# Causal attention of many small heads: every product of the groups in four column tiles, masks included

## The chip, the cores and the metric

One core of one Trainium2 chip runs the whole program. The metric is the device time in microseconds; the kernel before was timed in three runs.

## The reference

`x` is (2, 2048, 256) in f32, and the attention has 16 heads of 16 columns. Cut to what matters:

```python
Q, K, V = (proj(Wq), proj(Wk), proj(Wv))          # x @ W.T, split into 16 heads of 16
scores = scale * einsum('bhtd,bhsd->bhts', Q, kb)  # causal: -inf where s > t
m_new = maximum(m, max(scores)); p = exp(scores - m_new)
acc = corr * acc + einsum('bhts,bhsd->bhtd', p, vb)
x = layernorm(x + O @ Wo.T)
x = layernorm(x + int8_product(x, rhs))            # rows of x and columns of rhs quantised to 127
```

## The kernel before

**Groups.** The 32 heads (2 batches of 16) are worked through in 8 groups of 4 heads. The queries of a group lie in 4 chunks of 512 columns, the keys in 16 blocks of 128. Q and K are split into three bf16 parts and stacked, so that one bf16 product over 96 rows gives a score in f32 quality. Three more rows carry the negative maximum of each query, so that the product of scores (99 rows) already has it subtracted.

**Two kinds of product.** The *maxima* are made first: an item `(i, b, w, h)` of `ITEMS` is the product of the 128 queries of tile `i` with `w` keys of block `b`, for two heads (`PAIR`). It fills one of two slots (`MAX_SLOTS`) of two PSUM banks; VectorE reduces it to block maxima (L975). An item on the diagonal (`diag`, `b == i // TPC`) is 128, 256, 384 or 512 wide and gets a second matmul behind its product (L705), which adds -1e30 above the diagonal of its last 128 columns: `ident_b` times `mask_q`. A group has 80 items, 32 of them on the diagonal. The *scores* are made later, in 40 steps `(c, kb)` of `STEPS`, each for four heads: keys of one block in the rows, up to 512 queries in the columns (384, 256 and 128 in the last three steps of a chunk). They go through three PSUM banks; ScalarE takes the exponential into `PR` (L927). GpSimd cuts the diagonal (L1197).

**Values.** Two steps later (`LAG`) the four heads' values are multiplied in f32: four matmuls side by side in the four column tiles of the array, 32 columns of weights each, into one bank (L728). The trace shows an f32 matmul as two.

**Forms.** A matmul with 128 columns of weights uses the whole array. `product` can cut it into four matmuls with 32 columns of weights each (`QUADS`, `QW`), one beside the other in the four column tiles. Before, `in_quads` says which: 384 columns and wider, and never an item on the diagonal. So non-diagonal items (all 512 wide) and scores of 512 and 384 columns go in quarters (L688); diagonal items, their masks and scores of 256 and 128 columns go whole (L686, L705).

**Order.** TensorE's order is written out ahead by `quota`. It runs over the steps with a clock counted in columns, gives each product at least `LOAD` = 256 columns and each change of form `FORM` = 288, and places the next item behind a score when the item's slot is free. The stream of a *steady* group (the first six) is the items from 46 (`AHEAD`) on of its own, and the items before 46 of the next; the seventh (*full*) makes all 80 of the last group too, 114 in all; the last one makes none and has the end of the layer (projection, norms, integer product) beside it. In a steady group the planner finds a place for each item with the slot free when TensorE comes to it; in the seventh it has to let TensorE come up to 1024 columns earlier. When a chunk's items are done, TensorE turns the maxima (L713, whole), ScalarE negates them, GpSimd splits them into three parts and SP loads them into the stack (`TURNS`).

**Front.** Before the groups the weights and `x` are turned and projected; the first 46 items of group 0 lie in between (`FRONT_QUOTA`).

Of the kernel before, what the change touches and what calls it, by code (L numbers as in the profile page):

```python
# [26 lines left out]
P = 128  # L27
# [8 lines left out]
CH = 512  # L36
TPC = CH // P
# [4 lines left out]
MAX_SLOTS = 2  # L42
PAIR = 2
# [25 lines left out]
def build(nc, x, wq, wk, wv, wo, ffn, out):  # L69
# [8 lines left out]
    STACK = len(Q_TERMS) * DH  # L78
    KROWS = STACK + PARTS
# [8 lines left out]
    ITEMS = [(i, b, min(CH, P * (i + 1) - CH * b), h)  # L88
             for i in range(TILES) for b in range(i // TPC + 1) for h in range(HG // PAIR)]
    NI = len(ITEMS)  # L90
    ITEM_COLS = [PAIR * w for _, _, w, _ in ITEMS]
# [3 lines left out]
    skip = lambda c, kb: P * max(0, kb - TPC * c)  # L95
# [10 lines left out]
        full=[(0, n) for n in range(AHEAD, NI)] + [(1, n) for n in range(NI)],  # L106
        last=[])

    QUADS, WIDE = 4, 384
    QW = P // QUADS  # L110
    in_quads = lambda w, diag=False: w >= WIDE and not diag

    LAG, BATCH = 2, 1
    FORM, LOAD, READ, READ_FROM = 288, 256, 2.5, 340

    def quota(stream):

        made = lambda m: PAIR * (max(ITEM_COLS[m] // PAIR, LOAD) + (P if ITEMS[m][1] == ITEMS[m][0] // TPC else 0))  # L120
        read = lambda m: READ_FROM + READ * ITEM_COLS[m]

        def place(pace, early):
            at, done, free, seen, n, out, quads = 0, 0, [0] * MAX_SLOTS, 0, 0, [], True
            for k, (c, kb) in enumerate(STEPS):
                out.append([])
                for j in range(HG):
                    at += max(CH - skip(c, kb), LOAD) + FORM * (quads != in_quads(CH - skip(c, kb)))
                    quads = in_quads(CH - skip(c, kb))
                    if n < len(stream) and free[n % MAX_SLOTS] <= at + early and seen * pace <= at:  # L130
                        i, b, w, _ = ITEMS[stream[n][1]]
                        at = max(at, free[n % MAX_SLOTS]) + made(stream[n][1]) + FORM * (quads != in_quads(w, b == i // TPC))
                        quads = in_quads(w, b == i // TPC)
                        done = max(done, at) + read(stream[n][1])
                        free[n % MAX_SLOTS] = done
                        seen += read(stream[n][1])
                        n += 1
                    out[k].append(n)
                if k % BATCH == BATCH - 1:
                    at += FORM * (not quads)  # L140
                    quads = True
                    at += sum(HG * (CH - skip(*STEPS[k - back])) for back in range(LAG, LAG + BATCH))
            return out if n == len(stream) else None

        return next(out for early in range(0, 16 * CH, CH // 2) for pace in range(160, -1, -2)
                    for out in [place(pace / 100, early)] if out) if stream else [[0] * HG for _ in STEPS]
# [17 lines left out]
    FRONT_QUOTA, n, seen = [], 0, 0  # L164
# [77 lines left out]
    with ExitStack() as ctx:  # L242
# [9 lines left out]
        ident_b = sb("ident_b", [P, P], BF16)  # L252
        ones = sb("ones", [P, P], F32)
        mask_q = sb("mask_q", [P, P], BF16)
# [10 lines left out]
        QS = QS_words[:, :].bitcast(BF16).rearrange("p (s c j n) -> p s c j n", s=2, c=CHUNKS, j=HG)  # L265
        KS = sb("KS", [KROWS, 2, CHUNKS, HG, CH], BF16)
# [143 lines left out]
        with nc.Block() as block:  # L410
# [172 lines left out]
            def _(pe):  # L583
# [69 lines left out]
                def front():  # L653
                    pe.wait_ge(ready, 1)
                    turn_weights(0)
                    turn_x(0, 0)
                    turn_weights(1)
                    turn_x(0, 1)
                    turn_weights(2)
                    done = 0  # L660
                    for n in range(XCHUNKS):
                        for u in range(UNITS_X):
                            if n == 0 and u in (0, 2, 4):
                                pe.wait_ge(w_copied, u // 2 + 1)
                            unit(n, u)
                            if n == 0 and u == 3:
                                turn_weights(3)
                                turn_weights(4)
                            if n == 1 and u == 2:
                                ffn_weights()  # L670
                            if u in (1, 3) and n + 1 < XCHUNKS:
                                turn_x(n + 1, u // 2)
                            for m in range(done, FRONT_QUOTA[n][u]):
                                if m == 0:
                                    pe.wait_ge(ready, 2)
                                    pe.wait_ge(f_copied, 2)
                                item(0, 0, m)
                            done = FRONT_QUOTA[n][u]
                        if n == FRONT_TURN:
                            turn_first_maxima()  # L680

                def product(bank, w, stack, moving, quads, stop=True):


                    if not quads:
                        return pe.matmul(bank[:, 0:w], stack, moving, start=True, stop=stop)  # L686
                    for t in range(QUADS):
                        m = pe.matmul(bank[t * QW:t * QW + QW, 0:w], stack[:, t * QW:t * QW + QW], moving,  # L688
                                      start=True, stop=stop)
                    return m  # L690

                def item(q, p, n):

                    i, b, w, h = ITEMS[n]
                    if n in FIRST_ITEM:
                        pe.wait_ge(s_qs[p][i // TPC], SL * (q + 1))
                        pe.wait_ge(s_ks[p][i // TPC], SL * (q + 1))
                    at_least(pe, s_reduced, item_use(2 * q + p, n) - MAX_SLOTS + 1)
                    diag = b == i // TPC
                    for t in range(PAIR):  # L700
                        bank, j = ps_max[:, n % MAX_SLOTS * PAIR + t, :], h * PAIR + t
                        m = product(bank, w, QS[0:STACK, p, i // TPC, j, i % TPC * P:i % TPC * P + P],
                                    KS[0:STACK, p, b, j, 0:w], in_quads(w, diag), stop=not diag)
                        if diag:
                            m = pe.matmul(bank[:, w - P:w], ident_b[:, :], mask_q[:, :], start=False, stop=True)  # L705
                    m.then_inc(s_piece, 1)

# [24 lines left out]
                def group(q, p):  # L732
                    g, kind = 2 * q + p, KIND(2 * q + p)
                    first = isinstance(g, int) and g == 0
                    groups = [(q, p), (q, 1) if p == 0 else (q + 1, 0)]
                    n = 0
                    for k, (c, kb) in enumerate(STEPS):
                        s = skip(c, kb)
                        if kb == 0:
                            pe.wait_ge(s_qs[p][c], SL * (q + 1))  # L740
                            pe.wait_ge(s_ks[p][c], SL * (q + 1))
                            pe.wait_ge(s_mrow[c], 16 * PARTS * (g + 1))
                        for j in range(HG):
                            pos = unit_pos(kind, k, j)
                            at_least(pe, s_exp, score_base(g) + pos - behind(pos) + 1)
                            bank = ps_score[:, score_slot(pos), :]
                            product(bank, CH - s, KS[:, p, kb // TPC, j, kb % TPC * P:kb % TPC * P + P],
                                    QS[0:KROWS, p, c, j, s:CH], in_quads(CH - s)).then_inc(s_st, 1)
                            while n < QUOTA[kind][k][j]:
                                on, m = STREAM[kind][n]  # L750
                                item(*groups[on], m)
                                n += 1
                            if kind == "last" and j % 2:
                                project(k, j // 2)
                        if kind == "last":
                            end_parts(k)
                        if k >= LAG:
                            values(g, k - LAG, kind)
                        elif not first:
                            values(g - 1, NS + k - LAG, KIND(g - 1))  # L760
                        for at, on, tc in TURNS[kind]:
                            if at == k:
                                pos = turn_pos(kind, on, tc)
                                turn_maxima(g + on, tc, score_base(g) + pos, pos)
# [546 lines left out]
```

## Time and profile before

| | |
|---|---|
| median of three runs | 1074.32 us (1074.15 to 1074.58) |
| profiled execution | 1081.22 us |
| its span | 1079.5 us |
| TensorE, matmuls | 1014.5 us, 94% |
| VectorE | 826.0 us, 77% |
| ScalarE | 716.4 us, 66% |
| mean granted clock of TensorE | 0.978 |

The span is the stretch from the first to the last instruction of the profiled execution. A matmul's length in the timeline includes its way through the array, so lengths overlap; how fast matmuls follow each other is read from their starts. "PEld" is the loading of weights, "96*32" the rows and columns of the weights, "96x512" the rows and columns that stream past them. A line "x8" merges eight instructions: its length is from the first start to the last end.

### The profile page before, as it was taken

Reading aid. Unit: us, or ns where it says so; the run is one execution under the profiler, and the core shown is the slowest. Engines: PE = TensorE matmul, PEld = TensorE weight load, DVE = VectorE, ACT = ScalarE, POOL = GpSimd, SP = SyncE. Lnnn points to the kernel's source line nnn. Section 1 sums busy time; section 2 is a strip of 40 time slices with the busy share of each in tenths; the row PEclk is TensorE's granted clock in tenths of the full one; section 3 lists DMA queues with packets and bytes.
Section 4 is the critical chain, followed back from the end, with each engine's and each line's share of the span. In section 5 each row is a group of like instructions: output and inputs, shape, how many; then the busy total and the mean of one; then the engine's idle time right before and its main releaser. Section 6 shows DMA issues by size and latency. Waiting matters only on the chain.

```text
span 1079.5 us, 27959 instructions
## 1 busy us (share of the span) xinstructions
PE 1014.5 (94%) x11656; PEld 416.3 (39%) x11656; DVE 826.0 (77%) x1083; ACT 716.4 (66%) x1471; POOL 264.0 (24%) x435
## 2 busy tenths in 40 slices
PE   8999999999999999999999999999999899999872
PEld 5554433333333333333333333334333333434331
DVE  4566667877787778777877778777788898499697
ACT  3444477677767787777777777777766466677640
POOL 3534520112011201120112011101211101565644
PEclk9999989999999999999999999999999999999995
DMA  5656510003010301030103011201120410315501
GB/s 165 189 165 214 160 26 7 8 2 86 21 37 9 85 16 38 10 87 12 38 18 84 7 37 29 74 7 42 33 70 8 118 41 2 97 53 151 154 30 49
DMA packets 71810, 66.88 MB, mean 62 GB/s; under 512 B 15112, under 2 KB 65608, under 8 KB 71684
## 3 DMA queue, kind: packets, MB, share of 16 engines
q1 hardware_dynamic: 71684, 65.10, 21.5%
q8 instruction: 92, 1.51, 0.6%
q14 instruction: 34, 0.28, 0.1%
HBM read 43.25 MB, written 21.35 MB: 60 GB/s over the span
## 4 chain that ended last, share of the span: by engine, by line
PE 81%; DVE 10%; ACT 4%; DMA 2%; issue 1%; SPq 1%; POOL 1%; POOLq 0%; DVEq 0%; ACTq 0%
PE ps_acc L728 21%; PE ps_score L688 18%; PE ps_max L688 15%; PE ps_max L686 8%; DVE block_max L975 6%; PE ps_score L611 5%; ACT PR L927 3%; PE ps_score L686 3%; PE ps_max L705 3%; PE ps_score L618 3%; PE ps_max L802 2%; DMA end_slots<-heads_out 1%; PE ps_acc L592 1%; DVE stats L1089 1%; DMA row_sums<-accS 1%
## 5 line engine op out<-in xcount | busy, mean ns | idle before, releaser
L975 DVE TENSOR_REDUCE block_max<-ps_max 128x2 f32<-128x1024 f32 (+3 forms) x640 | 658.5, 1062 | 196.8 <-PE ps_max L688 108.4
L927 ACT ACTIVATE PR<-ps_score 128x512 f32<-128x512 f32 (+3 forms) x1280 | 628.1, 537 | 229.0 <-PE ps_score L688 142.4
L688 PE MATMUL ps_score<-QS,KS 99*32 99x512 bf16 (+1 forms) x4096 | 347.4, 377 | 12.8 <-ACT PR L927 10.6
L728 PE MATMUL ps_acc<-PR,VG 128*32 128x512 f32 (+3 forms) x2560 | 295.4, 536 | 0.0
L688 PE MATMUL ps_max<-KS,QS 96*32 96x512 bf16 x3072 | 236.1, 383 | 10.9 <-DVE block_max L975 8.5
L1197 POOL TENSOR_SCALAR_AFFINE_SELECT PR<-PR 128x512 f32<-128x512 f32 x128 | 81.6, 638 | 456.3 <-ACT PR L927 456.3
L688 PEld LDWEIGHTS ps_score<-QS,KS 99*32 99x32 bf16 x4096 | 104.7, 95 | 202.4 <-ACT PR L927 94.4
L686 PE MATMUL ps_max<-KS,QS 96*128 96x384 bf16 (+3 forms) x512 | 128.8, 305 | 3.5 <-DVE block_max L975 2.8
L688 PEld LDWEIGHTS ps_max<-KS,QS 96*32 96x32 bf16 x3072 | 68.8, 96 | 109.2 <-DVE block_max L975 51.8
L705 PE MATMUL ps_max<-mask_q,ident_b 128*128 128x128 bf16 x512 | 102.8, 221 | 0.0
L728 PEld LDWEIGHTS ps_acc<-PR,VG 128*32 128x32 f32 x2560 | 68.0, 109 | 49.2 <-issue 10.6
L686 PEld LDWEIGHTS ps_max<-KS,QS 96*128 96x128 bf16 x512 | 48.9, 98 | 97.0 <-issue 45.2
L611 PE MATMUL ps_score<-PR,wT 128*128 128x512 f32 x128 | 62.3, 613 | 0.7 <-ACT neg_max L889 0.7
L686 PE MATMUL ps_score<-QS,KS 99*128 99x256 bf16 (+1 forms) x256 | 54.7, 257 | 3.3 <-ACT PR L927 1.7
L1184 POOL TENSOR_TENSOR end_slots<-PR,end_slots 128x512 bf16<-128x512 f32 x32 | 37.0, 1157 | 70.0 <-ACT end_slots L876 70.0
L686 PEld LDWEIGHTS ps_score<-QS,KS 99*128 99x128 bf16 x256 | 21.2, 98 | 84.0 <-ACT PR L927 70.6
L871 ACT CAST end_slots<-ps_score 128x512 bf16<-128x512 f32 x32 | 18.8, 586 | 49.4 <-PE ps_score L611 49.4
L705 PEld LDWEIGHTS ps_max<-mask_q,ident_b 128*128 128x128 bf16 x512 | 50.4, 99 | 2.8 <-issue 2.3
L1205 POOL CAST max_parts<-neg_max 16x128 bf16<-16x128 f32 (+1 forms) x31 | 8.8, 285 | 127.4 <-ACT neg_max L910 125.8
L1189 POOL COPY VG<-V 128x256 f32<-128x256 f32 x32 | 12.7, 396 | 87.3 <-PE ps_acc L728 87.0
L611 PEld LDWEIGHTS ps_score<-PR,wT 128*128 128x128 f32 x128 | 22.4, 192 | 24.8 <-issue 24.0
L618 PE MATMUL ps_score<-wT,PR 128*128 128x256 f32 x128 | 31.0, 387 | 0.0
(126 smaller groups left out, 550.1 us busy)
## 6 DMA issues: line engine op xcount, KB each, us to landing
QS<-qparts SPq DMA_DIRECT2D x192, 64.0 KB, 2.4
KS<-kparts SPq DMA_DIRECT2D x192, 64.0 KB, 2.4
qparts<-end_slots SPq DMA_DIRECT2D x16, 384.0 KB, 5.0
kparts<-end_slots SPq DMA_DIRECT2D x16, 384.0 KB, 4.6
PR<-in_L_attn_x SPq DMA_DIRECT2D x8, 512.0 KB, 4.6
heads_out<-accS SPq DMA_DIRECT2D x124, 32.0 KB
end_slots<-in_L_attn_x SPq DMA_DIRECT2D x4, 512.0 KB, 9.5
out_y<-end_slots SPq DMA_DIRECT2D x8, 256.0 KB, 2.1
```

The lines of the kernel that those rows point to most:

```text
L611: m = pe.matmul(bank, wT[:, w, mh, nh * P:nh * P + P], xT[:, n % 2, mh, :], start=mh == 0, stop=mh == HALVES - 1)
L618: m = pe.matmul(bank[:, t * D:t * D + D], xT[:, n % 2, mh, tile * P:tile * P + P], wT[:, 2, mh, :], start=mh == 0, stop=mh == HALVES - 1)
L686: return pe.matmul(bank[:, 0:w], stack, moving, start=True, stop=stop)
L688: m = pe.matmul(bank[t * QW:t * QW + QW, 0:w], stack[:, t * QW:t * QW + QW], moving, start=True, stop=stop)
L705: m = pe.matmul(bank[:, w - P:w], ident_b[:, :], mask_q[:, :], start=False, stop=True)
L728: m = pe.matmul(ps_acc[EYE * j:EYE * j + EYE, s:CH], VG[:, kb, j, :], PR[:, k % 4, j, 0:CH - s], start=kb == 0, stop=k == LAST[c])
L802: y = pe.matmul(ps_max[:, s, t * D:t * D + D], o_in(m)[:, h, at:at + P], wT[:, 3, h, :], start=h == 0, stop=h == HALVES - 1)
L871: act.copy(parts[:, n % 2, u, 0, :], ps_score[:, u % 3, :]).then_inc(part1, 1)
L927: act.activation(PR[:, k % 4, j, 0:w], ps_score[:, score_slot(pos), 0:w], ACT.Exp, scale=SCALE).then_inc(s_exp, 1)
L975: dve.tensor_reduce(block_max[:, h * PAIR:h * PAIR + PAIR, i, b], ps_max[:, slot_at:slot_at + PAIR, 0:w], AX.X, ALU.max).then_inc(s_reduce ...
L1184: pool.tensor_tensor(parts[:, n % 2, u, 2, :], rest[:, q % RESTS, :], parts[:, n % 2, u, 1, :], ALU.subtract).then_inc(part3, 1)
L1197: pool.affine_select(out=block, in_=block, compare_op=ALU.is_ge, fill=0.0, base=0, pattern=[[0, HG], [1, P]], channel_multiplier=-1).then_ ...
```

## The change

All products of the groups go in quarters, whatever their width, and the mask of a diagonal item goes in quarters too. Quarter `r` of the mask covers the rows from `r` and the columns from its own diagonal on, so the four are 128, 96, 64 and 32 columns wide. The items in the front stay whole (`quads=False`). The planner loses the price of a change of form and counts a mask as `LOAD` = 256 columns instead of 128; with this its order shifts by an item here and there, and two turns of maxima of a steady group come one step later (22 to 23, 29 to 30).

```diff
--- before.py
+++ after.py
@@ -106,39 +106,33 @@
         full=[(0, n) for n in range(AHEAD, NI)] + [(1, n) for n in range(NI)],
         last=[])
 
-    QUADS, WIDE = 4, 384
+    QUADS = 4
     QW = P // QUADS
-    in_quads = lambda w, diag=False: w >= WIDE and not diag
 
     LAG, BATCH = 2, 1
-    FORM, LOAD, READ, READ_FROM = 288, 256, 2.5, 340
+    LOAD, READ, READ_FROM = 256, 2.5, 340
 
     def quota(stream):
 
 
 
-        made = lambda m: PAIR * (max(ITEM_COLS[m] // PAIR, LOAD) + (P if ITEMS[m][1] == ITEMS[m][0] // TPC else 0))
+        made = lambda m: PAIR * (max(ITEM_COLS[m] // PAIR, LOAD) + (LOAD if ITEMS[m][1] == ITEMS[m][0] // TPC else 0))
         read = lambda m: READ_FROM + READ * ITEM_COLS[m]
 
         def place(pace, early):
-            at, done, free, seen, n, out, quads = 0, 0, [0] * MAX_SLOTS, 0, 0, [], True
+            at, done, free, seen, n, out = 0, 0, [0] * MAX_SLOTS, 0, 0, []
             for k, (c, kb) in enumerate(STEPS):
                 out.append([])
                 for j in range(HG):
-                    at += max(CH - skip(c, kb), LOAD) + FORM * (quads != in_quads(CH - skip(c, kb)))
-                    quads = in_quads(CH - skip(c, kb))
+                    at += max(CH - skip(c, kb), LOAD)
                     if n < len(stream) and free[n % MAX_SLOTS] <= at + early and seen * pace <= at:
-                        i, b, w, _ = ITEMS[stream[n][1]]
-                        at = max(at, free[n % MAX_SLOTS]) + made(stream[n][1]) + FORM * (quads != in_quads(w, b == i // TPC))
-                        quads = in_quads(w, b == i // TPC)
+                        at = max(at, free[n % MAX_SLOTS]) + made(stream[n][1])
                         done = max(done, at) + read(stream[n][1])
                         free[n % MAX_SLOTS] = done
                         seen += read(stream[n][1])
                         n += 1
                     out[k].append(n)
                 if k % BATCH == BATCH - 1:
-                    at += FORM * (not quads)
-                    quads = True
                     at += sum(HG * (CH - skip(*STEPS[k - back])) for back in range(LAG, LAG + BATCH))
             return out if n == len(stream) else None
 
@@ -674,12 +668,12 @@
                                 if m == 0:
                                     pe.wait_ge(ready, 2)
                                     pe.wait_ge(f_copied, 2)
-                                item(0, 0, m)
+                                item(0, 0, m, quads=False)
                             done = FRONT_QUOTA[n][u]
                         if n == FRONT_TURN:
                             turn_first_maxima()
 
-                def product(bank, w, stack, moving, quads, stop=True):
+                def product(bank, w, stack, moving, quads=True, stop=True):
 
 
                     if not quads:
@@ -689,7 +683,7 @@
                                       start=True, stop=stop)
                     return m
 
-                def item(q, p, n):
+                def item(q, p, n, quads=True):
 
                     i, b, w, h = ITEMS[n]
                     if n in FIRST_ITEM:
@@ -700,8 +694,12 @@
                     for t in range(PAIR):
                         bank, j = ps_max[:, n % MAX_SLOTS * PAIR + t, :], h * PAIR + t
                         m = product(bank, w, QS[0:STACK, p, i // TPC, j, i % TPC * P:i % TPC * P + P],
-                                    KS[0:STACK, p, b, j, 0:w], in_quads(w, diag), stop=not diag)
-                        if diag:
+                                    KS[0:STACK, p, b, j, 0:w], quads, stop=not diag)
+                        if diag and quads:
+                            for r in range(0, P, QW):
+                                m = pe.matmul(bank[r:r + QW, w - P + r:w], ident_b[:, r:r + QW], mask_q[:, r:P],
+                                              start=False, stop=True)
+                        elif diag:
                             m = pe.matmul(bank[:, w - P:w], ident_b[:, :], mask_q[:, :], start=False, stop=True)
                     m.then_inc(s_piece, 1)
 
@@ -745,7 +743,7 @@
                             at_least(pe, s_exp, score_base(g) + pos - behind(pos) + 1)
                             bank = ps_score[:, score_slot(pos), :]
                             product(bank, CH - s, KS[:, p, kb // TPC, j, kb % TPC * P:kb % TPC * P + P],
-                                    QS[0:KROWS, p, c, j, s:CH], in_quads(CH - s)).then_inc(s_st, 1)
+                                    QS[0:KROWS, p, c, j, s:CH]).then_inc(s_st, 1)
                             while n < QUOTA[kind][k][j]:
                                 on, m = STREAM[kind][n]
                                 item(*groups[on], m)
```

## Rows read from the trace of the kernel before

**Rows 1.** Busy time of each engine over the span, from the page.

```profile
PE 1014.5 (94%) x11656; PEld 416.3 (39%) x11656; DVE 826.0 (77%) x1083; ACT 716.4 (66%) x1471; POOL 264.0 (24%) x435
```

**Rows 2.** The chain that ended last, by engine and by line.

```profile
PE 81%; DVE 10%; ACT 4%; DMA 2%; issue 1%; SPq 1%; POOL 1%; POOLq 0%; DVEq 0%; ACTq 0%
PE ps_acc L728 21%; PE ps_score L688 18%; PE ps_max L688 15%; PE ps_max L686 8%; DVE block_max L975 6%; PE ps_score L611 5%; ACT PR L927 3%; PE ps_score L686 3%; PE ps_max L705 3%; PE ps_score L618 3%; PE ps_max L802 2%; DMA end_slots<-heads_out 1%; PE ps_acc L592 1%; DVE stats L1089 1%; DMA row_sums<-accS 1%
```

**Rows 3.** A steady group, the seventh and the eighth: length, busy us (instructions), clock, DMA share, GB/s.

```profile
core 0: us, PE busy (x) PEld busy (x) DVE busy (x) ACT busy (x) POOL busy (x), PEclk, DMA share, GB/s
459.90:566.40 106.50, 105.36 (x1381) 40.63 (x1381) 83.29 (x85) 80.95 (x169) 17.12 (x36) 1.00 0.14 37
779.70:917.50 137.80, 125.54 (x1589) 46.64 (x1588) 116.92 (x125) 83.49 (x169) 17.54 (x37) 0.99 0.19 49
917.50:1045.40 127.90, 116.34 (x1062) 51.09 (x1061) 102.63 (x278) 85.85 (x186) 72.34 (x102) 0.97 0.37 100
```

**Rows 4.** The timeline of TensorE: start us, length us, line, what, [idle before].

```profile
start us, us, engine line op out<-in xcount [idle before <-releaser]
...
499.78 0.60 PE L688 MATMUL ps_max<-KS,QS 96*32 96x512 bf16 x8
500.21 0.60 PE L688 MATMUL ps_score<-QS,KS 99*32 99x512 bf16 x8
...
503.91 1.03 PE L728 MATMUL ps_acc<-PR,VG 128*32 128x512 f32 x8
504.77 0.39 PE L688 MATMUL ps_score<-QS,KS 99*32 99x512 bf16 x4
505.10 0.23 PE L686 MATMUL ps_max<-KS,QS 96*128 96x128 bf16 x1
505.16 0.22 PE L705 MATMUL ps_max<-mask_q,ident_b 128*128 128x128 bf16 x1
505.22 0.22 PE L686 MATMUL ps_max<-KS,QS 96*128 96x128 bf16 x1
505.28 0.22 PE L705 MATMUL ps_max<-mask_q,ident_b 128*128 128x128 bf16 x1
505.43 0.40 PE L688 MATMUL ps_score<-QS,KS 99*32 99x512 bf16 x4
```

**Rows 5.** The narrow values: their timeline row, and their group by form (mean ns of one).

```profile
353.00 0.39 PE L728 MATMUL ps_acc<-PR,VG 128*32 128x128 f32 x8
...
L728 PE MATMUL ps_acc<-PR,VG 128*32 128x128 f32 x256 | 12.9, 276 | 0.0
```

**Rows 6.** Weight loads by form: xcount | busy us, mean ns of one | idle before.

```profile
L688 PEld LDWEIGHTS ps_score<-QS,KS 99*32 99x32 bf16 x4096 | 104.7, 95 | 202.4 <-ACT PR L927 94.4 <-issue 54.7 <-POOL KS L1277 1.8
...
L728 PEld LDWEIGHTS ps_acc<-PR,VG 128*32 128x32 f32 x2560 | 68.0, 109 | 49.2 <-issue 10.6 <-ACT PR L927 6.1
...
L611 PEld LDWEIGHTS ps_score<-PR,wT 128*128 128x128 f32 x128 | 22.4, 192 | 24.8 <-issue 24.0 <-DVE PR L1024 0.2
```

**Rows 7.** VectorE's timeline: four pairs of 512 columns together, and one alone.

```profile
482.11 4.71 DVE L975 TENSOR_REDUCE block_max<-ps_max 128x2 f32<-128x1024 f32 x4 [1.10 <-PE ps_max L688]
...
502.59 1.23 DVE L975 TENSOR_REDUCE block_max<-ps_max 128x2 f32<-128x1024 f32 x1 [0.45 <-PE ps_max L705]
```

**Rows 8.** Who waited for whom in the steady group: us in total, times, longest.

```profile
ACT PR L927 <- PE ps_score L688: 13.1, 33, 1.1
DVE block_max L975 <- PE ps_max L688: 12.5, 20, 1.1
PEld ps_score L688 <- ACT PR L927: 10.2, 32, 0.9
DVE block_max L975 <- PE ps_max L705: 9.6, 17, 1.3
```

**Rows 9.** Two stretches with many instructions of TensorE, columns as in rows 3.

```profile
271.61:274.89 3.28, 3.28 (x64) 1.57 (x64) 3.28 (x3) 3.09 (x7) 0.00 (x0) 1.00 0.15 45
357.19:364.90 7.71, 7.62 (x126) 3.33 (x127) 6.22 (x7) 6.55 (x15) 0.98 (x2) 1.00 0.07 14
```

## The prediction

> **What bounds the kernel now.** I read the busy shares first, then the chain, then the stretches group by group, and last the timeline of TensorE alone. TensorE is busy for 94% of the span, VectorE for 77%, ScalarE for 66% [rows 1], and 81% of the chain that ended last lies on TensorE, 10% on VectorE [rows 2]. The busy share hides what the engine does with its time, so I cut out three stretches [rows 3]: one steady group of heads (106.5 us; six groups of eight are of this kind), the seventh group, which makes the maxima of two groups (137.8 us), and the eighth, with the end of the layer beside it (127.9 us). In the steady one VectorE is busy 83.3 us and ScalarE 81.0 us of 106.5.
>
> The timeline shows what the time of TensorE consists of. Products in quarters, 512 columns wide, go at 0.215 us each: two of them begin at 499.78 and the next line at 500.21. A step of values has two passes of 0.43 us (503.91 to 504.77) [rows 4]. Whole products go at their width too: the 128-wide ones and their masks start every 0.06 us. But each change of form costs: score in quarters at 504.77, whole product at 505.10, that is 0.33 where the columns need 0.215, so 0.11 into the whole form; last mask at 505.28, quarters at 505.43, 0.15 where 0.06 is needed, so 0.09 back. A pair costs 0.20 us, and this repeats for every diagonal item between two scores [rows 4].
>
> Steady group, from the widths and counts in the kernel and these starts: 208 products in quarters of 512 and 16 whole ones at 0.217 = 48.6; 32 of 384 at 0.165 = 5.3; 32 of 256 at 0.111 = 3.6; 32 of 128 at 0.058 = 1.9; 64 masks at 0.059 = 3.8; values 28 x 0.86 + 4 x (0.65 + 0.43 + 0.22) = 29.3; four turns 0.4. Together 92.9 us. Following the planner's order by hand I count 98 changes of form (turns of maxima are whole), at 0.10 = 9.8. So 102.7 us of work and 3.8 of waiting. By the same count the seventh group has 107.5 us of columns, 112 changes (11.2) and 19 us of waiting; the eighth has 16 changes.
>
> **The change, part by part.**
>
> *Changes of form.* After it only the turns are whole: 8 changes in a steady group, 8 in the seventh, 4 in the eighth. Removed: 6 x 90 + 104 + 12 = 656, at 0.10 us = 66 us of TensorE work. In a steady group it is 9.0 us, in the seventh 10.4, in the eighth 1.2.
>
> *Narrow products and masks in quarters.* Per steady group 16 scores and 16 products of maxima 128 wide and 64 masks, in all six steady groups 576; the seventh has 120, the eighth 16: 712 pieces that now go at 0.06 us. The trace shows no bf16 quarter narrower than 384. Lower bound: the columns, 0.058 us as whole (the mask's quarters are 128, 96, 64 and 32 wide, all beside each other, so the longest counts), a cost of nothing. Upper bound: the nearest row of narrow quarters, the values of 128 columns in f32. Eight matmuls take 0.39 us where one takes 0.276, so a pass of four with its four weight loads takes 0.11 us [rows 5]. That row's columns alone explain its 0.11, so it is an upper bound only. Between them I weigh the weight loads. One of 128 columns f32 takes 192 ns and one of 32 takes 109: 0.86 ns a column. With 32 columns bf16 it takes 95, which is 14 less than f32, so 0.44 ns a column [rows 6]. Four loads of 32 bf16 columns one behind the other are then 56 ns, just within the 58 of the columns. I take 0.06 us: 1 us in all. The other end is 712 x 0.054 = 38 us. Products of 256 columns (0.111) fit under either price.
>
> The Trainium skill, "TensorEngine Tiling (Array Packing)", section Restrictions, says that column tiling switches off the fast weight load, and "TensorE: Matmul & The Clock Gate", section LDWEIGHTS, gives a load as its columns over 1.2 GHz; four loads of 32 columns would be 107 ns, an estimate from that page, and the sum would be that of the first rival. The load durations of the trace speak for half of that per column.
>
> *First maxima whole.* The items in the front keep their form and the front (to about 133 us) stays as it is: nothing.
>
> *The planner's order.* Prices without changes of form shift some items by one score and two turns of maxima by one step (22 to 23, 29 to 30 in a steady group). GpSimd's split, SP's three loads of rows and the scores that need them follow 14 and more steps later; at some 2.6 us a step they are covered. If that cover were gone, it would cost one step a group, 2.6 us. Each piece put in quarters has four matmuls and four weight loads in place of one and one: more instructions, the third rival.
>
> *What is late next.* VectorE and ScalarE do the same work in less time. Steady: TensorE's work is 92.9 + 0.8 (eight changes) + 0.2 = 93.9 us. Without more waiting the group takes 97.7. With VectorE at 83.3 and only two buffer slots more waits must come. VectorE's 512-wide pairs follow each other at 1.16 us when it is fed (four in 4.71, one lasts 1.23) [rows 7], so its own floor is about 80. The two stretches bound the waits: 3.8 us (3.6%) where VectorE has 19% less work than TensorE, and 19 us (14%) in the seventh group, where they have nearly the same (116.9 against 118.7). At 11% less a straight line between gives 8.2%, 102.3 us. I choose nearer to the steady end, 5.6 us, for the planner places a steady item only where its slot is free by its own count, while the seventh group's order lets TensorE come up to 1024 columns early, so part of those waits is planned. Steady: 99.5 us, 7.0 saved, x 6 = 42. Seventh: TensorE's 10.4 go, VectorE's 116.9 stay; I keep half, 5. Eighth: of 1.2 us 1, since ScalarE and the end parts hold it. Together 48 us.
>
> The profiled execution took 1081.2 us (span 1079.5), 6.9 over the median of the timed runs; the saving is the same for both: 1074.3 - 48 = 1026, and with 1 us for narrow pieces 1027.
>
> **Rivals.**
>
> *1. A narrow quarter product costs 0.11 us.* For it: the planner itself gives every product at least 256 columns, and f32 quarters were never seen quicker. Against it: the weight loads above, and whole narrow products at 0.06 against the same planner price. Steady group: 96 x 0.054 = 5.2 more, 99.1 of work and 3.5 of waiting, 102.6; 3.9 x 6 = 23, seventh 2, eighth 0: 1049.
>
> *2. VectorE and ScalarE take the time back.* By the straight line a steady group needs 102.3 us: 25 saved, 3 in the seventh: 1046. By the seventh group's share of 14%, it would be 109, that is nothing saved or a little lost. Against it: in the steady group VectorE still waits for TensorE, 12.5 and 9.6 us, while TensorE's waits for it are too short to be among the largest [rows 8].
>
> *3. The instruction stream becomes the bound, and it is slower.* A steady group has 2,762 matmuls and weight loads before [rows 3] and 3,722 after (32 scores, 64 products, 64 masks, six more each). At 106.5 us that is 28.6 ns each: should TensorE's sequencer feed slower than this over a whole group, the kernel is slower. Today's mean is 38.6 ns, and the densest stretches that I found are 128 in 3.28 us (25.6 ns) and 253 in 7.71 us (30.5 ns) [rows 9]. At 30.5 ns a steady group would take 113.5, + 7 x 6 = 42: 1116. For it: nothing in the trace shows a longer stretch at 26 ns, and the new order has stretches of 512 at about 20. Against it: in both stretches TensorE ran at its column rate without a gap, so nothing shows the feed as the limit either.
>
> *4. More is saved:* no new waits, all in the seventh group: 54 + 9 + 1: 1010.
>
> **How the numbers follow.** Forecast (1012 to 1036) 0.52; rival 1 0.17; rival 2 0.14, a third of it at no change; rival 3 0.10; rival 4 0.07. Range 1010 to 1056: it takes in the forecast, rival 1 and the milder part of rival 2 and ends at the gain of rival 4. Within 0.2% (2 us), about what a measurement of this kernel can tell from no change: 0.05. Slower 0.11 (rival 3 and a little of 2). Faster 0.84.
>
> **What would show it.** Starts of 128-wide quarters every 0.06 us (right) or every 0.11 (rival 1); from a 512-wide score to a 128-wide item 0.22 instead of 0.33; steady group near 99.5 us. TensorE's waits for VectorE above 8 us a group would be rival 2; idle time of TensorE put down to "issue", with all buffers free, rival 3. The prediction is wrong if the four narrow matmuls don't run beside each other or if the masks' accumulation onto the columns just written makes them wait: neither is seen in quarters before.

## The result, and the profile after

The changed kernel takes 1022.36 us (four runs, 1021.68 to 1023.52) against 1074.24 us before (four runs, 1073.15 to 1074.58): a ratio of 0.952, 95% interval 0.9503 to 0.9536. That is 51.9 us saved where 48 (less 1) were forecast. The busy shares and the chain, from the page of the changed kernel, answer to [rows 1, 2]:

```profile
PE 944.3 (93%) x15088; PEld 475.6 (47%) x15088; DVE 822.7 (81%) x1083; ACT 708.1 (69%) x1471; POOL 263.5 (26%) x435
...
PE 70%; DVE 16%; ACT 7%; issue 3%; DMA 2%; POOL 1%; SPq 1%; POOLq 0%; DVEq 0%; ACTq 0%
```

TensorE has 29% more matmuls and is busy 70 us less. VectorE does the same work in less time, and its part of the chain has grown from 10% to 16%: it is what comes next. With its reads halved, further below, the changed kernel takes another 26 us less.

The same three stretches as in [rows 3], cut at the same points of the program: a steady group, the seventh, the eighth.

```profile
428.30:527.80 99.50, 97.03 (x1860) 49.15 (x1861) 82.75 (x85) 79.65 (x170) 17.10 (x36) 1.00 0.16 41
727.40:860.20 132.80, 118.82 (x2165) 51.88 (x2164) 116.77 (x125) 83.11 (x169) 17.54 (x37) 0.99 0.21 52
860.20:985.80 125.60, 114.20 (x1158) 50.57 (x1157) 102.78 (x278) 85.80 (x186) 72.11 (x102) 1.00 0.38 102
```

The steady group went from 106.5 to 99.5 us, the seventh from 137.8 to 132.8, with all instructions of the new forms in place (1,860 matmuls and 1,861 weight loads in the steady one).

TensorE's timeline around a 128-wide item on the diagonal, to be read against [rows 4]:

```profile
436.61 0.40 PE L682 MATMUL ps_score<-QS,KS 99*32 99x512 bf16 x4
436.83 0.23 PE L682 MATMUL ps_max<-KS,QS 96*32 96x128 bf16 x4
436.89 0.22 PE L700 MATMUL ps_max<-mask_q,ident_b 128*32 128x128 bf16 x4
436.93 0.24 PE L682 MATMUL ps_max<-KS,QS 96*32 96x128 bf16 x4
436.98 0.24 PE L700 MATMUL ps_max<-mask_q,ident_b 128*32 128x32 bf16 x4
437.10 0.40 PE L682 MATMUL ps_score<-QS,KS 99*32 99x512 bf16 x4
```

From the score to the item it is now 0.22 us (436.61 to 436.83) instead of 0.33, and from the last mask to the next score 0.12 (436.98 to 437.10) instead of 0.15. A narrow product in quarters and its mask start 0.06 us after each other, as whole ones did. From score to score with such an item between it is 0.49 us; it was 0.66. That is 0.17 less, not the full 0.20 of two changes, because the item itself takes 0.27 us (436.83 to 437.10) for its four pieces where 0.24 was reckoned. The first product's masks start at 436.89 and the next product already at 436.93, too soon for one that waits behind a mask of 128 columns (0.06). It begins where a tile is already free, and the next line, whose first mask is the 32-wide one, fits with this.

Who waited for whom in the steady group, against [rows 8]. A row gives the time waited in us, how often, and the longest; first the changed kernel:

```profile
ACT PR L925 <- PE ps_score L682: 15.1, 40, 1.1
PEld ps_score L682 <- ACT PR L925: 12.7, 39, 0.9
...
DVE block_max L973 <- PE ps_max L682: 9.1, 22, 1.0
...
DVE block_max L973 <- PE ps_max L700: 6.4, 11, 1.3
PEld ps_max L682 <- DVE block_max L973: 5.8, 17, 0.6
```

Of the kernel before, the rows that answer to the last one and stand lower down than [rows 8] shows:

```profile
PEld ps_score L686 <- ACT PR L927: 9.0, 17, 0.8
...
PEld ps_max L688 <- DVE block_max L975: 4.1, 13, 0.4
PEld ps_max L686 <- DVE block_max L975: 3.7, 9, 0.6
```

VectorE's waits for TensorE went from 22.1 to 15.5 us. TensorE's weight loads waited 7.8 us for a slot that VectorE still read (4.1 and 3.7, on two lines), and 5.8 in the changed kernel. So this row doesn't show VectorE holding TensorE more than before: a load can wait while the matmul ahead of it still runs, and then it costs nothing. What VectorE holds is read from the kernels with half reads, below.

The profiled executions differ by more (1081.2 and 1021.7 us) than the medians. In that of before the granted clock was 0.59 from 132 to 144 us, that is near the lower of TensorE's two levels (1.2 GHz) for most of this stretch; in that of the changed kernel it was 1.00 there:

```profile
132.00:144.00 12.00, 11.25 (x80) 2.89 (x80) 5.82 (x7) 5.72 (x14) 3.96 (x8) 0.59 0.35 98
```

Before it fell TensorE had stood still for 1.27 us at the first score. In the changed kernel it stood still there for 1.69 us and the clock stayed; but in a second profile of the changed kernel, after the same 1.69 us, it fell too (0.72 from 126 to 132 us, 1.00 behind). Of the ten profiles below and here whose front is that of the changed kernel, all with this stop of 1.69 us, five have a fall there and five have none. So the length of the stop doesn't decide it. Stretches are compared below, or medians, not spans.

### The profile page after: what moved, and what is told of

Same layout as the page of the kernel before. It is cut to its first block, busy times and chain, and to the rows that moved or that the text cites. A ratio compares the mean times of both kernels' runs of the same rounds, so it can differ in the third digit from the quotient of the medians.

```text
span 1019.9 us, 34823 instructions
## 1 busy us (share of the span) xinstructions
PE 944.3 (93%) x15088; PEld 475.6 (47%) x15088; DVE 822.7 (81%) x1083; ACT 708.1 (69%) x1471; POOL 263.5 (26%) x435
## 4 chain that ended last, share of the span: by engine, by line
PE 70%; DVE 16%; ACT 7%; issue 3%; DMA 2%; POOL 1%; SPq 1%; POOLq 0%; DVEq 0%; ACTq 0%
PE ps_acc L726 19%; PE ps_max L682 18%; PE ps_score L682 17%; DVE block_max L973 10%; PE ps_score L605 6%; ACT PR L925 5%; PE ps_score L612 3%; PE ps_max L700 2%; PE ps_max L800 2%; PE ps_max L680 2%; DMA end_slots<-heads_out 1%; DVE stats L1087 1%; ACT accS L913 1%; PE ps_acc L586 1%; DMA PR<-in_L_attn_x 0%
## 5 line engine op out<-in xcount | busy, mean ns | idle before, releaser
L682 PE MATMUL ps_score<-QS,KS 99*32 99x512 bf16 (+3 forms) x5120 | 418.0, 349 | 20.2 <-ACT PR L925 15.1
L682 PE MATMUL ps_max<-KS,QS 96*32 96x512 bf16 (+3 forms) x4752 | 346.5, 349 | 16.8 <-DVE block_max L973 13.3
L682 PEld LDWEIGHTS ps_score<-QS,KS 99*32 99x32 bf16 x5120 | 153.6, 95 | 215.7 <-ACT PR L925 114.4
L682 PEld LDWEIGHTS ps_max<-KS,QS 96*32 96x32 bf16 x4752 | 133.2, 96 | 155.4 <-DVE block_max L973 73.5
L700 PE MATMUL ps_max<-mask_q,ident_b 128*32 128x96 bf16 (+3 forms) x1872 | 102.4, 200 | 1.8 <-issue 1.8
L700 PEld LDWEIGHTS ps_max<-mask_q,ident_b 128*32 128x32 bf16 x1872 | 61.1, 97 | 12.1 <-issue 2.0
L1022 DVE TENSOR_TENSOR PR<-ps_score,end_slots 128x512 f32<-128x512 f32 x32 | 21.8, 683 | 8.3 <-ACT end_slots L869 7.2
L680 PE MATMUL ps_max<-KS,QS 96*128 96x512 bf16 (+3 forms) x92 | 24.1, 338 | 2.6 <-issue 2.1
L612 PEld LDWEIGHTS ps_score<-wT,PR 128*128 128x128 f32 x128 | 23.8, 190 | 4.1
L913 ACT COPY accS<-ps_acc 128x512 f32<-128x512 f32 x32 | 19.4, 608 | 8.8 <-PE ps_acc L726 8.7
```

Of the source, the lines that this page charges most:

```text
L612: m = pe.matmul(bank[:, t * D:t * D + D], xT[:, n % 2, mh, tile * P:tile * P + P], wT[:, 2, mh, :], start=mh == 0, stop=mh == HALVES - 1)
L700: m = pe.matmul(bank[r:r + QW, w - P + r:w], ident_b[:, r:r + QW], mask_q[:, r:P], start=False, stop=True)
L913: act.copy(accS[:, c % 2, :], ps_acc[:, :]).then_inc(s_accS, 1)
L1022: dve.tensor_tensor(rest[:, q % RESTS, :], ps_score[:, u % 3, :], parts[:, n % 2, u, 0, :], ALU.subtract)\
```

## The experiments

**The kernel before, once more**, for a second profile.

> The kernel before, once more, for its profile only. In the first profile TensorE's clock fell to half around the start of the first group (0.50 from 135 to 143 us) and the profiled execution was 6.9 us over the median. If that was a chance of one execution, this profile's span is near 1073 us with the clock at 1.0 there; if it belongs to the kernel, the fall is there again and the change also gained by avoiding it.

1079.45 us, span 1077.7. The clock was 0.58 in the same stretch, so the fall is not of one execution alone; but in the kernel before with half reads, below, whose order there is the same, it was 1.00. The mean granted clock was 0.978 and 0.980 in the two profiles of before; of eleven timed runs beside this one nine have 0.982 to 0.988 and take 1072 to 1077 us, and two have 0.978 and 0.980 and take 1079 to 1080. The median of 1074 is therefore one without the long fall, and the 51.9 us are not owed to it. Steady group and seventh repeat: 106.4 and 137.9 us.

**The front's items in their old form.**

```diff
-                                item(0, 0, m, quads=False)
+                                item(0, 0, m, quads=ITEMS[m][1] < ITEMS[m][0] // TPC)
```

> The changed kernel, but the 24 items of the front off the diagonal go in quarters again, as before the change (the 22 on the diagonal stay whole). Theory: between the whole f32 products of the front each such item costs two changes of form, 24 x 0.20 = 4.8 us, which the prediction left out: 1022.4 + 4.8 = 1027. Rival: TensorE waits for others in the front anyway, and the front gives nothing: 1022.

1026.72 us (1024.52 to 1029.15), ratio to before 0.9548 (0.9521 to 0.9575): 4.4 us more than the changed kernel, where the theory said 4.8. The timeline of TensorE shows the price of it. This kernel:

```profile
127.26 1.99 PE L612 MATMUL ps_score<-wT,PR 128*128 128x256 f32 x8
129.18 0.61 PE L682 MATMUL ps_max<-KS,QS 96*32 96x512 bf16 x8
129.73 1.99 PE L612 MATMUL ps_score<-wT,PR 128*128 128x256 f32 x8
```

The changed kernel in the same part:

```profile
120.27 1.89 PE L612 MATMUL ps_score<-wT,PR 128*128 128x256 f32 x8
122.00 0.60 PE L680 MATMUL ps_max<-KS,QS 96*128 96x512 bf16 x2
122.43 1.89 PE L612 MATMUL ps_score<-wT,PR 128*128 128x256 f32 x8
```

From one f32 product to the next with an item between: 2.47 us in the one, 2.16 in the other. A pair of changes beside f32 products costs 0.31 us, more than the 0.20 between bf16 ones; 24 x 0.31 = 7.4 us of TensorE, of which 4.4 showed in the medians. The profiles put it somewhat higher: with the front of before the first score starts at 131.6 to 133.5 us (four profiles), with that of the changed kernel at 124.5 to 128.8 (ten), and the means are 6.3 us apart.

**The old order with the new forms**: the planner of before, unchanged (`FORM`, `in_quads` and the mask at `P` columns in `quota`), all else as in the changed kernel.

> The changed kernel with the planner of before (its price for changes of form, masks at 128 columns), so that only the forms differ from the kernel before. Theory: the order is worth next to nothing, 1022 to 1025. Rival: a part of the 52 us comes from the new order; then this is above 1030.

1023.22 us (1021.45 to 1027.67), steady group 99.7 us against 99.5. The new order is worth 0.2 us a group at most, which is no more than a measurement can tell; the gain is that of the forms.

**Forms put back in part, in the same order.** Three kernels, each with one kind whole again: the scores under 384 columns; the items on the diagonal; only the masks.

```diff
-                                    QS[0:KROWS, p, c, j, s:CH]).then_inc(s_st, 1)
+                                    QS[0:KROWS, p, c, j, s:CH], CH - s >= 384).then_inc(s_st, 1)
```

> The changed kernel, but scores of 256 and 128 columns whole, in the same order: 332 changes of form instead of 60 by count. Theory (0.10 us a change, a quarter of it taken out of waits that are there anyway): 272 x 0.10 x 0.75 = 20 us more, 1043. If narrow quarters had cost more than whole ones (rival 1 of the prediction, 0.05 us on 128 products 128 wide) 6 us of this would come back: 1036.

```diff
                     diag = b == i // TPC
+                    quads = quads and not diag
```

> The changed kernel, but items on the diagonal whole with their masks, scores all in quarters, same order: 528 changes of form instead of 60. Theory: 468 x 0.10 x 0.75 = 35 us more, 1057. With the run that has the scores whole (20 more) it should account for the 47 that the groups gave.

```diff
-                        if diag and quads:
+                        if diag and quads and False:
```

> The changed kernel, but only the masks whole (one matmul of 128 x 128), products in quarters, same order: 996 changes of form instead of 60. Theory (0.10 us a change): 936 x 0.10 = 94 us more on TensorE; at the share of 0.75 that shows it is 70, so 1092, up to 1116 if all shows: slower than the kernel before either way. Rival: it is the number of instructions or narrow pieces that matters, not the changes; then with fewer instructions this is not over 1030.

| kernel | changes of form in a steady group (counted) | steady group, us | median, us | ratio to before |
|---|---|---|---|---|
| changed | 8 | 99.5 | 1022.36 | 0.952 |
| scores whole | 44 | 102.3 | 1037.74 | 0.9656 (0.9622 to 0.969) |
| diagonal items whole | 72 | 104.0 | 1051.10 | 0.9771 (0.9743 to 0.98) |
| before | 98 | 106.5 | 1074.24 | 1 |
| masks whole | 136 | 110.7 | 1101.83 | 1.0247 (1.0218 to 1.0276) |

Each ratio is against runs of the kernel before on the same chip. The group's length rises with the count of changes, whichever kind is put back, and not with that of instructions: 0.078, 0.070, 0.078 and 0.088 us for each change above 8. The kernel with whole masks has fewer instructions than the changed one (1,669 against 1,860 matmuls in the group) and the same narrow products, and is slower than before. Its timeline shows why:

```profile
474.78 0.23 PE L682 MATMUL ps_max<-KS,QS 96*32 96x128 bf16 x4
474.94 0.23 PE L703 MATMUL ps_max<-mask_q,ident_b 128*128 128x128 bf16 x1
475.10 0.24 PE L682 MATMUL ps_max<-KS,QS 96*32 96x128 bf16 x4
475.28 0.23 PE L703 MATMUL ps_max<-mask_q,ident_b 128*128 128x128 bf16 x1
```

Product and mask start 0.16 us apart instead of 0.06: 0.10 for each change. The scores alone gave 15 us where 20 were expected, the items 29 where it was 35, the masks 79 (70 to 94): the mechanism is right, the share that shows was set a little high for the first two. Scores and items together give 44 of the 47 us that the groups gave.

**Masks over all 128 columns in each quarter.**

```diff
-                                m = pe.matmul(bank[r:r + QW, w - P + r:w], ident_b[:, r:r + QW], mask_q[:, r:P],
+                                m = pe.matmul(bank[r:r + QW, w - P:w], ident_b[:, r:r + QW], mask_q[:, :],
```

> The changed kernel, but each quarter of a mask over all 128 columns instead of 128, 96, 64 and 32 (the values added are the same). Theory: the quarters run beside each other and the first one, 128 wide in both, sets the time: 1022, no change beyond 1 us. Rival: the quarters share the stream, so that columns saved in three of them count as an average of 48 of 128: 468 x 0.02 = 9 us more, 1031.

1018.18 us (1016.91 to 1025.31), ratio 0.948 (0.9451 to 0.951), which overlaps the changed kernel's; the median is 4 us below where none or 1 was expected, but the steady group has 99.5 us in both. The triangular cut of the masks is worth nothing here. In the timeline of this kernel the next product starts 0.06 us behind the mask, not 0.04, and the next score 0.26 us behind the start of the item, against 0.27:

```profile
439.29 0.23 PE L700 MATMUL ps_max<-mask_q,ident_b 128*32 128x128 bf16 x4
439.35 0.23 PE L682 MATMUL ps_max<-KS,QS 96*32 96x128 bf16 x4
439.40 0.23 PE L700 MATMUL ps_max<-mask_q,ident_b 128*32 128x128 bf16 x4
439.49 0.40 PE L682 MATMUL ps_score<-QS,KS 99*32 99x512 bf16 x4
```

The tiles with a short mask run ahead in the changed kernel, but the first tile has 128 columns in both.

**More instructions for the same columns.** Each 512-wide product without a mask in two halves of 256 columns:

```diff
+                    if w == CH and stop:
+                        for x in range(0, w, w // 2):
+                            for t in range(QUADS):
+                                m = pe.matmul(bank[t * QW:t * QW + QW, x:x + w // 2], stack[:, t * QW:t * QW + QW],
+                                              moving[:, x:x + w // 2], start=True, stop=stop)
+                        return m
```

> The changed kernel, but every product of 512 columns without a mask (scores and items off the diagonal) in two halves of 256 columns, so eight quarters instead of four: some 1,660 more matmuls and weight loads in a steady group (3,722 to 5,386). Theory: the feed of instructions has room, and each product costs one more gap of about 5 ns: some 1,650 products x 0.005 = 8 us more, 1031. Rival 3 of the prediction: if the sequencer can't feed at 18.5 ns an instruction, a steady group goes well over 104 us; at 25 ns it would be 135 us and the kernel near 1240.

1027.47 us (1024.82 to 1030.16): 5 us more, where 8 were expected. Its steady group:

```profile
428.90:528.70 99.80, 97.37 (x2692) 67.66 (x2693) 82.77 (x85) 79.74 (x170) 17.11 (x36) 1.00 0.15 40
```

5,385 matmuls and weight loads in 99.8 us, 18.5 ns each, against 26.7 in the changed kernel: 0.3 us more for 1,664 more instructions. The feed of instructions (rival 3) is no bound in a steady group. In the seventh it is not so free. There TensorE stands still three times, 5.5 us in all, and the profile puts it down to "issue", the sign that the prediction named for rival 3; this is the last and longest of them:

```profile
816.23 0.40 PE L684 MATMUL ps_score<-QS,KS 99*32 99x256 bf16 x4 [3.01 <-issue]
```

The changed kernel has two such stops there in its first profile (1.28 and 1.80 us) and none in its second:

```profile
804.26 0.41 PE L726 MATMUL ps_acc<-PR,VG 128*32 128x256 f32 x2 [1.28 <-issue]
...
813.01 0.22 PE L700 MATMUL ps_max<-mask_q,ident_b 128*32 128x128 bf16 x4 [1.80 <-issue]
```

The two profiles of the kernel before have none in their groups. So in one group, and not in every execution, the added instructions cost up to 3 us in the changed kernel.

**VectorE's work halved**, in the changed kernel and in that of before (the maxima of the second half of each item's columns are left out):

```diff
-                    dve.tensor_reduce(block_max[:, h * PAIR:h * PAIR + PAIR, i, b], ps_max[:, slot_at:slot_at + PAIR, 0:w],
+                    dve.tensor_reduce(block_max[:, h * PAIR:h * PAIR + PAIR, i, b], ps_max[:, slot_at:slot_at + PAIR, 0:w // 2],
```

> The changed kernel, but VectorE reduces only the first half of an item's columns (the maxima of the other half are left out), so VectorE's work on items falls to nearly half and is no limit. Theory: TensorE's work alone remains, 94 to 95 us in a steady group, about 109 to 112 in the seventh: 1022 - 6 x 5 - 22 = 970. Rival: the waits are ScalarE's (three score banks), then a steady group stays over 98 us.

> The kernel before with the same half reads of VectorE (half of each item's columns left out of the maxima). Theory: 103 to 104 us in a steady group, about 120 in the seventh: 1074 - 6 x 3 - 18 = 1038. Against the changed kernel with half reads that is 66 us or more, the whole price of the 656 changes of form: then the missing part of it was held by VectorE. Rival: the pair differs by the same 52 us as with full reads; then the price of a change is 0.075 us and nothing was held.

994.59 us (989.75 to 998.2) and 1060.66 us (1057.23 to 1063.46). Both are well over what was expected (970 and 1038), but they differ by 66.1 us, not by 52. A steady group and the seventh of the changed kernel with half reads:

```profile
421.40:518.50 97.10, 95.73 (x1861) 53.85 (x1860) 49.25 (x85) 79.49 (x169) 17.18 (x36) 1.00 0.16 42
...
713.40:831.00 117.60, 111.42 (x2165) 63.14 (x2164) 69.92 (x124) 82.47 (x169) 17.60 (x37) 0.99 0.26 60
```

Of the kernel before with half reads:

```profile
454.10:560.30 106.20, 105.21 (x1381) 40.77 (x1381) 49.44 (x84) 80.93 (x169) 17.12 (x36) 1.00 0.14 37
...
773.00:896.10 123.10, 120.02 (x1589) 48.09 (x1588) 70.47 (x124) 83.49 (x169) 17.55 (x37) 1.00 0.22 55
```

With VectorE's work halved the steady group differs by 9.1 us for 90 changes, the full 0.10 each. VectorE held 0.3 us of a steady group before and 2.4 after. Some 3.2 and 3.5 us stay that are not in the sum of the work (97.1 and 106.2 against 93.9 and 102.7). In the changed kernel little of this is VectorE's, since the weight loads now wait only 1.4 us for it, where it was 5.8. The largest wait left on TensorE's side is that of the weight loads for ScalarE:

```profile
PEld ps_score L682 <- ACT PR L925: 12.5, 38, 0.9
```

It was 12.7 us with full reads, and much of it lies behind running matmuls. That ScalarE causes the 3.2 us, as the rival has it, is likely and not shown: no run makes ScalarE faster.

In the seventh group the pair differs by 5.5 us though 104 changes (10.4 us) are gone. The trace of the changed kernel with half reads shows where the other 5 are: two stops of "issue", 2.31 and 1.13 us, and a fall of the clock behind the first.

```profile
780.23 0.41 PE L726 MATMUL ps_acc<-PR,VG 128*32 128x256 f32 x2 [2.31 <-issue]
...
777.90:780.20 2.30, 0.01 (x1) 0.00 (x0) 0.07 (x1) 0.18 (x1) 0.00 (x0) 1.00 1.07 267
780.20:788.30 8.10, 8.07 (x127) 5.29 (x127) 3.50 (x6) 5.52 (x11) 0.00 (x0) 0.79 0.98 178
```

The stops are 3.4 us, and 8.1 us at a mean clock of 0.79 cost another 1.7 (an estimate: 0.21 x 8.1). Without them, and without the one stop of 0.4 us in the kernel before with half reads, the pair would differ by 10.2. That the two totals differ by 66 us, the number forecast, is in part luck: 6 x 9.1 = 55 in the steady groups and 5.5 in the seventh are less than forecast, and the front, which the forecast left out, makes up for it.

**True prices in the planner**, beside the changed kernel on the same chip.

```diff
-    LOAD, READ, READ_FROM = 256, 2.5, 340
+    LOAD, READ, READ_FROM = 128, 2.5, 340
```

> The changed kernel once more, on the chip of the runs beside it, to compare with the one of true prices. Expected 1022, steady group 99.5 us; if the seventh group's length (132.8 us in its first profile, 131.5 and 129.2 in two runs whose code is the same or nearly the same there) moves by 2 us or more again, that group has a spread of its own.

> The changed kernel, but the planner counts a product and a mask as at least 128 columns instead of 256, which is what the narrow quarters now cost in the profile (0.06 us). The forms are the same, only items and turns move. Theory: items are spaced by a clock that runs 3 us slow in a steady group, so TensorE comes early and waits; with the true price a part of the 5.6 us of waiting goes, 98.5 us a steady group and 1016 in all. Rival: VectorE's two slots set the waits whatever the spacing, 1022; or items come closer and TensorE waits more, up to 1027.

1012.98 us (1010.6 to 1015.64), ratio to before 0.9427 (0.9395 to 0.9458), against 1020.44 (1017.66 to 1025.96) and 0.9494 (0.9462 to 0.9526) for the changed kernel: 7 us less (6 were expected), with intervals that just part. A steady group takes 98.4 us instead of 99.5, the seventh 129.2 against 129.3:

```profile
427.20:525.60 98.40, 96.38 (x1860) 52.09 (x1860) 82.57 (x85) 79.74 (x169) 17.06 (x36) 1.00 0.16 42
723.30:852.50 129.20, 118.13 (x2165) 53.12 (x2164) 116.07 (x125) 82.39 (x170) 17.54 (x37) 0.99 0.21 53
```

This beats both kernels; 6 x 1.1 us in the steady groups is nearly all of it. The changed kernel's second profile has the same steady group (99.5) and a seventh of 129.3 us where the first had 132.8: the two stops of "issue", 3.1 of these 3.5 us, are in the first only. So the seventh group's part in the gain of the change (137.8 before) is 5.0 us with the stops and 8.5 without.

## Why the prediction was right, step by step

**Price of a change of form: right.** 0.10 us read off the starts [rows 4]; with VectorE's work halved 90 changes less give 9.1 us, and whole masks put 0.10 us between product and mask.

**Narrow quarters at 0.06 us: right; rival 1 wrong.** They start 0.06 us apart (0.27 for the four pieces of a 128-wide item with its masks), and the steady group has no 5.2 us more. The four weight loads of 32 columns add nothing that shows in these starts. "TensorE: Matmul & The Clock Gate" in the Trainium skill, section LDWEIGHTS, would have them take 107 ns one behind the other (an estimate from that page); by that rule, each pair would start 0.11 us apart, and the trace disagrees: 436.83 to 436.89.

**Waits: right in size, with luck in it.** 99.5 us less 93.9 of work is 5.6 us, the very value chosen between 3.8 and 8.4. But it was chosen by judgement: no row fixed it, the straight line through the two stretches gave 8.4, and another choice between the two would have been as well founded. The half reads show whose the waits are: 2.4 us VectorE's and 3.2 not. In the prediction all that was added (1.8) was VectorE's, which the runs confirm (0.3 before, 2.4 after); rival 2 in its straight-line form would have been 102.3. The sign that was named for rival 2, waits of TensorE for VectorE above 8 us a group, could hardly tell: they were 7.8 us on the weight loads before the change.

**Seventh group: 5 forecast, 5.0 and 8.5 measured.** The forecast let VectorE keep half of the 10.4 us. Without the stops of "issue" 8.5 show, so 2 are kept back and not half; that the first profile has just 5.0 is luck, for the rest went into stops that the prediction knew only as rival 3. **Eighth: 1 forecast;** its stretch lasted 127.9 us before (125.4 in the second profile: 918.2 to 1043.6 us) and 125.6 and 126.0 after, which tells nothing apart.

**The front: wrong.** The step said "The items in the front keep their form [...]: nothing", and the section on the change has them "stay whole". They did not: 24 of the 46, those off the diagonal, had gone in quarters, by `in_quads`, between whole f32 products, and `quads=False` made them whole. The first score, from which the front's end is read, started at 132.75 us before (131.87 in the second profile) and at 126.44 and 127.59 after. Put back, they cost 4.4 us. The price there is 0.31 us a pair, not 0.20. This is nearly the whole difference between the 47 us forecast with the narrow pieces and the 51.9 measured.

**Order of the planner: nothing**, as said: 0.2 us a group. **Instruction feed (rival 3): wrong for the steady groups,** by 18.5 ns an instruction with 0.3 us lost, and its 1116 us with it; right in a small way in the seventh, up to 3 us.

The sum of the stretches: steady groups 6 x 7.0 = 42, seventh 5.0 to 8.5, front 4.4 to 6.3, the eighth near 0: 51 to 57, measured 51.9 and, on the second chip, 53.4.

## What to carry to other kernels

Where an engine is busy 94% of the time, read the starts, not the lengths: a fixed gap wherever the kind of instruction changes (here 0.10 us, 0.31 a pair beside f32) is work that can be taken away, even at the price of four times the instructions. When the limit moves, set the planner's prices anew: they were worth 7 us here. And for every default that a diff changes, ask which callers had the old behaviour: the front's 24 items were in no list of what the change touches, and gave 4.4 of the 51.9 us. When a group varies from profile to profile, look for the stops in it before calling it a spread.

## What the runs showed of the hardware that was not expected

Column tiles keep their own time. Where quarters have unequal widths, later matmuls of one tile start before earlier ones of another: after masks of 128, 96, 64 and 32 columns the second set starts with the 32-wide one. These rows of the changed kernel's first group show it, a score (issued later) starting before the 128-wide mask of another tile:

```profile
128.33 0.33 PE L682 MATMUL ps_score<-QS,KS 99*32 99x384 bf16 x1
...
128.37 0.22 PE L700 MATMUL ps_max<-mask_q,ident_b 128*32 128x128 bf16 x1
```

A change of form beside f32 products costs more than beside bf16: a product of eight f32 matmuls takes 1.92 us to the next start behind it when it stands between changes and 1.73 when it doesn't. The weight load of 128 f32 columns lasts 192 ns [rows 6] and would no longer be hidden; that this is the cause was not tried.

TensorE can stand still with nothing in the profile to wait for. All stops of "issue" over 0.5 us within the groups lie in the seventh. Five of the eleven profiles of the changed kernel and its variants have them (the first of the changed kernel, those with the front's items in their old form, with wide masks, with halves and with half reads), and none of the three of the kernel before, with full or half reads. They begin while SP loads `QS` and `KS`: the share of the DMA engines was 1.06 in the first stop of the changed kernel, 1.07 in that of the half reads, and lower in the later ones (0.38 in the second of the changed kernel). Between two stops the same number of instructions goes through, 127 matmuls and 127 weight loads, here in the changed kernel and in that with halves:

```profile
804.30:811.10 6.80, 6.72 (x127) 3.32 (x127) 5.48 (x6) 5.33 (x10) 0.00 (x0) 1.00 0.86 161
...
808.80:813.20 4.40, 4.40 (x127) 3.23 (x127) 3.52 (x4) 3.53 (x7) 0.00 (x0) 1.00 0.71 164
```

The profile has a DMA queue called "instruction", with three packets from 790 to 820 us in the changed kernel. So the likely reading is that instructions come in blocks over the same DMA engines as the data, and that a block is now and then late there. It is not shown: no run moved the loads to try it.
